# Scores right behind the values' products, gates' parts ahead of the last copies, first tiles and shared weights handed over earlier

## The reference

```
x = x + tanh(g_xattn) * mlstm(layernorm(x), ctx, ctx)
x = x + tanh(g_ffn)   * experts(layernorm(x))

mlstm (16 heads of 32):
    ig = [q,k,v] @ Wi + bi ;  fg = [q,k,v] @ Wf + bf
    log_D = cumsum(log_sigmoid(fg)) differences + ig   (lower triangle)
    D  = exp(log_D - rowmax(log_D))
    C  = (q k^T / sqrt(32)) * D
    h  = C / max(|sum C|, exp(-rowmax)) @ v ; normalised per head, times ln_scale

experts: scores = sqrt(softplus(x @ gate_w^T)), the two best of 16 per token,
    y = w1*E_a(x) + w2*E_b(x) + shared(x),  E(x) = (silu(x W1^T) * (x W3^T)) W2^T
```

## Time and profile before

| | |
|---|---|
| median of 3 runs | 775.14 us (774.03 to 776.44) |
| the profiled execution, its own time | 775.68 us |
| its span, first to last instruction | 773.9 us |
| PE busy | 691.8 us (89%) |
| DVE, ACT, POOL busy | 506.0, 411.1, 392.3 us |
| mean granted TensorE clock | 0.974 |
| front stage, to its barrier | up to about 85.5 us |
| attention | up to about 299 us |
| mixture | the rest |

### The profile page before, as it was taken

How to read it: one execution, slowest core, us unless ns; L and a number is a source line. 1 busy time by engine, 2 the same in 40 slices (tenths; PEclk the granted TensorE clock), 3 DMA queues, 4 the chain that set the end, 5 groups by cost and what they waited for, 6 DMA issues and landing times.

```text
span 773.9 us, 19573 instructions
## 1 busy us (share of the span) xinstructions
PE 691.8 (89%) x7407; PEld 603.0 (78%) x7408; DVE 506.0 (65%) x1007; ACT 411.1 (53%) x851; POOL 392.3 (51%) x592
## 2 busy tenths in 40 slices
PE   0877498899899887999999999999999999999994
PEld 0644377777777766778899998999999999999993
DVE  4758278987777698866259795534566676766650
ACT  0667467686766674434362332223466656666651
POOL 2410377888888774521112542223355766667554
PEclk9999699999999998999999999999999999999998
DMA  7885464446555710687633222423678888979864
GB/s 248 276 277 173 120 191 142 155 143 183 143 161 168 229 41 28 203 303 277 236 104 110 59 86 75 118 88 105 200 223 237 226 257 229 238 225 240 256 130 54
DMA packets 90212, 134.55 MB, mean 174 GB/s; under 512 B 16704, under 2 KB 43840, under 8 KB 90144
## 3 DMA queue, kind: packets, MB, share of 16 engines
q1 hardware_dynamic: 73472, 106.04, 42.9%
q0 software_dynamic: 7168, 17.04, 11.1%
q10 hardware_dynamic: 9504, 10.55, 4.4%
HBM read 92.06 MB, written 33.95 MB: 163 GB/s over the span
## 4 chain that ended last, share of the span: by engine, by line
PE 68%; DVE 8%; ACT 4%; DMA 4%; issue 3%; POOL 1%; SPq 0%; ACTq 0%; POOLq 0%; DVEq 0%
PE psH L1302 30%; PE psY L1322 15%; PE psQ L719 4%; PE ring L736 4%; PE psO L764 4%; PE ring L704 2%; PE ring L730 2%; ACT dec L806 2%; PE psT L1282 2%; DMA out<-ystage,sidx 1%; DMA xT<-over13l 1%; DVE dec L886 1%; PE psR L1349 1%; DVE xl L1551 1%; ACT sq L830 1%
## 5 line engine op out<-in xcount | busy, mean ns | idle before, releaser
L1302 PE MATMUL psH<-xh,w13h 128*128 128x256 f32 (+1 forms) x768 | 220.8, 288 | 2.8 <-issue 2.8
L1302 PE MATMUL psH<-xh,w13l 128*128 128x256 f32 (+1 forms) x768 | 215.5, 281 | 0.0
L1302 PE MATMUL psH<-xl,w13h 128*128 128x256 f32 (+1 forms) x768 | 215.1, 280 | 0.0
L1794 POOL TENSOR_TENSOR hl<-sg,hh 128x256 fp32r<-128x256 f32 (+1 forms) x96 | 79.5, 837 | 177.9 <-ACT hh L1425 177.4
L1302 PEld LDWEIGHTS psH<-xh,w13h 128*128 128x128 f32 (+1 forms) x768 | 138.0, 180 | 11.3 <-issue 10.4
L1302 PEld LDWEIGHTS psH<-xl,w13h 128*128 128x128 f32 (+1 forms) x768 | 138.3, 180 | 0.8
L1302 PEld LDWEIGHTS psH<-xh,w13l 128*128 128x128 f32 (+1 forms) x768 | 138.0, 180 | 0.0
L886 DVE SCALAR_TENSOR_TENSOR dec<-psQ,dec 128x512 f32<-128x512 f32 x128 | 79.5, 683 | 44.2 <-PE psQ L719 44.1
L1420 ACT ACTIVATE sg<-psH 128x256 f32<-128x256 f32 (+1 forms) x96 | 36.4, 379 | 126.0 <-PE psH L1302 125.3
L1557 DVE TENSOR_TENSOR sg<-sg,psH 128x256 f32<-128x256 f32 (+1 forms) x96 | 40.0, 416 | 95.4 <-ACT sg L1420 95.4
L806 ACT ACTIVATE dec<-ring 128x512 f32<-128x512 f32 x128 | 71.2, 596 | 17.6 <-PE ring L707 17.1
(11 more groups left out here) (228 smaller groups left out, 1410.5 us busy)
## 6 DMA issues: line engine op xcount, KB each, us to landing
raw<-w13T SPq DMA_DIRECT2D x64, 352.0 KB, 4.4
gcT<-ctxT ACTq DMA_DIRECT2D x8, 1024.0 KB, 6.1
kT<-ctxT SPq DMA_DIRECT2D x16, 512.0 KB, 4.2
ctxs<-ctx SPq DMA_DIRECT2D x16, 512.0 KB, 3.8
xn<-xnorm SPq DMA_DIRECT2D x16, 512.0 KB, 3.3
out<-xres SPq DMA_DIRECT2D x16, 512.0 KB, 4.9
raw<-w2T SPq DMA_DIRECT2D x16, 512.0 KB
qst<-qT_all SPq DMA_DIRECT2D x14, 512.0 KB, 5.0
```

What stands on the lines that cost most here:

```text
L1302: last = nc.tensor.matmul(psH[m][0:n, v, :], w[wp][:, c, col:col + n], x[xp][:, c, :], start=(c == 0 and k == 0), stop=(c == DC - 1 and k ...
L1794: nc.gpsimd.tensor_tensor(hs[u.p][1][0:n, m, :], sg[0:n, m, :], hs[u.p][0][0:n, m, :].bitcast(F32), ALU.subtract).then_inc(hl_ready, 1)
```

## The change

Three places change.

1. In the front stage's last pair VectorE, not ScalarE, copies `xT`, and the copies to `qT_all` come after VectorE's last gate steps. ScalarE makes its second part ahead of the sums and the third ahead of the last `keep`. SyncE's last `store` follows the saving of all parts. VectorE alone fills both masks.
2. In attention `queries` comes right behind `values`, then `gather_state`, then the decays 2 and 3. The lists of the other engines stay.
3. At the end of attention SyncE starts the shared expert's quarters one at a time, at five places of sequences 13 to 15, where before all six transfers went out together. TensorE turns the first tile ahead of the last `values` and the second behind it, ahead of the last `back`. ScalarE and VectorE follow: VectorE normalises the first two tiles one step earlier and the next two after its last `take`.

```
@@ front_stage
+            for out, rows in ((g.aml[1], maskl), (g.amr[1], maskr)):
+                copy(out[:, :, :], rows[:, :].rearrange("p (o t) -> p o t", o=1).broadcast_to([P, NH, P]))
...
-            for n, _ in enumerate(gates_saved(sp, gt, half, 0, d)):
-                if n == 1:
-                    store(sp, 7)
+            for _ in gates_saved(sp, gt, half, 0, d):
+                pass
+            store(sp, 7)
...
-                    dve.wait_ge(xt_ready, n + 1)
+                    dve.wait_ge(turned, n + 1)
+                    dve.wait_ge(projected, n - 1)
+                    nc.vector.tensor_copy(xT[k][:, :, :], psT[k][:, :, :]).then_inc(xt_ready, 1)
+                for _ in gates:
+                    pass
+                for k in range(2):
+                    n = 2 * p + k
                     nc.vector.tensor_copy(g.qT_all[:, (n - 2) * DC:(n - 1) * DC, :], psT[k][:, :, :])
...
-                second_set(dve, nc.vector.tensor_copy, g.amr[1], maskr)
+                second_set(dve, nc.vector.tensor_copy)
@@ attention_stage, sync
                 load_em(b)
+                if b > B - 3:
+                    next(more)
...
                     sp.wait_ge(q_in[1], 16 * (B // 2 - 2))
+                if b >= B - 3:
                     next(more)
@@ attention_stage, tensor
                     values(i, r - 1, bank(r, OUT))
+                queries(i, r)
+                if r % 2 == 1:
+                    gather_state(i, r)
                 for k in range(2):
                     ring_free(use(last2(r) + k))
                     decay(i, r, 2 + k, bank(r, last2(r) + k))
-                    if k == 0:
-                        if r % 2 == 1:
-                            gather_state(i, r)
-                        queries(i, r)
...
             i, r = LAST
+            pe.wait_ge(c_done, 4 * NT)
+            next(more)
             ring_free(uses(i, r, END))
@@ mixture_stage, sync
                     sync.dma_start(raw13[:, c, :], src).then_inc(w_in[c], 16)
+                    if wset == 0:
+                        yield
@@ mixture_stage, vector
-            for count, quarters in ((2, ()), (2, ()), (0, (0, 1)), (2, (2,)), (2, (3,))):
+            for count, quarters in ((2, ()), (2, ()), (2, (0, 1)), (0, (2,))):
                 side.issue(-1, count)
                 split13(early(0), quarters)
-                if quarters == (3,):
-                    for j in range(2):
-                        split_x(early(0), j)
-                yield
+                yield
+            split13(early(0), (3,))
+            for j in range(2):
+                split_x(early(0), j)
+            yield
+            side.issue(-1, 2)
```

40 lines of the change are left out of this document (18 added, 22 removed).

## The result

The changed kernel takes 777.98 us (median of 6 runs, 777.33 to 781.73), the kernel before 776.02 beside it (6 runs, 774.03 to 778.89). The ratio on record is 1.0057, with a 95% interval of 1.0031 to 1.0083: **slower by 4.4 us**, between 2.4 and 6.4, where 2.95 us less was forecast. It is not the quotient of the two medians, which lie only 2.0 us apart. The median of 777.98 is outside the range of 769.0 to 776.5. In what follows ratios are turned into us in the same way, and each carries an uncertainty of about 2 us; the lengths of single steps in the traces are far sharper.

A forecast was written before the change was run, and what follows sets the result against it. TensorE, without gaps after 331 us, was taken as the bound, earlier gains arriving one to one: -4.5 + 4.45 - 2.7 - 0.2 = -2.95 us against 775.68; the median, 0.54 lower, gives 772.2 us, range 769.0 to 776.5.

The forecast's parts named there:

- Front end, -4.5: Front stage's end: masks saved and ready at 80.95 instead of 85.44 us, a gain of 4.5 us.
- Even steps, "so nothing": Attention's even steps: scores ahead of the decays start VectorE about 0.44 us earlier, nothing waits for it, so no change.
- Odd steps, +0.6 each: Attention's odd steps: state's sums behind the scores delay ScalarE's copies, 0.6 us more each, 5.4 over nine steps.
- First step, -0.75: Attention's very first step: scores no longer wait for a quarter of decays, which takes 0.7 there; gain 0.75 us.
- Weights, -2.7: Shared expert's weights near sequence 14: loading by quarters removes a 1.15 us wait and 1.6 of slow clock, gain 2.7 us.
- Rival (c): Weights' loads: decays still land late or the load moves beside other transfers, losing the 2.7 gain: 774.9 us; chance 0.17.
- Hand-over, -0.2: End of attention to the experts: late weighings against a faster way to `xl`, net gain 0.2 us, 1.7 if the clock holds.
- then 0.9 for the tiles: VectorE's first two normalisations at the end of attention, after waiting for GpSimd's power: priced at 0.9 us for both.
- The faster way from values 31 to the first `psH`: Tail: first tile turned and split under the last `values`; second `xl` ends at 298.05 in place of 299.2, -1.1 us.
- the clock falls behind the long gap: TensorE ahead of chunk 30's `values`: idle for 2.6 us, after which its clock falls to 1.2 GHz.
- Rival (b), the clock falls inside attention: Attention's odd steps: gaps grow to 1.2 us and each clock fall costs 1.6; four falls give 778.6 us; chance 0.07.
- The rule that the forecast set against this part: TensorE in attention: short idle times with PSUM banks in rotation can move the clock, so odd steps lose over 0.6 us.

The follow-up runs named there:

- `odd_gather_first`: The changed kernel with hand-over and even steps as before, and the state's sums right behind `values` in odd steps: ratio 0.9979 to the kernel before.

## Why the prediction was wrong, point by point

- **Front end, -4.5:** right, -4.5 measured alone (-2.8 to -6.2), and 4.7 at the end of the masks over all traces; by the steps that were named.
- **Even steps, "so nothing":** wrong, +1.4. The corner's product had been free beside the scores, a cost that the forecast put at nothing.
- **Odd steps, +0.6 each:** mechanism and size right: 5.0 for 5.4, 1.0 for 0.9, 0.66 for 0.45. Steps 29 and 31, left out, add 0.2.
- **First step, -0.75:** right in sign, 0.45. With this and the even steps the order adds up to +5.8 by the traces and +6.1 by the runs, and not +4.45.
- **Weights, -2.7:** in the trace exactly so, but on average 1.3 alone, and nothing beside the earlier front end. The term was read from one execution of a disturbance that came out between nothing and 3.8 us. Rival (c) named this loss, for a wrong reason: the decays do land in time.
- **Hand-over, -0.2:** the step that failed is "then 0.9 for the tiles": 2.64 beside GpSimd's wide instructions. That is 1.7 us more than it was priced at, and the weighing starts 3.85 us later, not 2.0. The faster way from values 31 to the first `psH` was right (4.77 us for 8.78), but with the late weighings `psH` comes 0.7 us late against values 29 in the changed kernel and not 1.1 early. With the hand-over alone values 31 are 5.2 us late against values 29, and 2.2 of this is given back by the last instruction. Net +3.0 in that trace, +2.6 by the runs. That the clock falls behind the long gap was right.
- **Rival (b), the clock falls inside attention:** did not happen; it is 1.00 in all stretches from 97 to 284 that I read. The rule that the forecast set against this part (the Trainium skill, TensorE: Matmul & The Clock Gate, A second HAM failure mode: psum-queue depth-cycling) decided nothing: TensorE's gap ahead of `values` did not double (0.65 us at 199.71 for 0.58 at 199.96), a second one of 0.44 came ahead of `back` instead, and at such gaps the clock held. Where a gap was longer, 1.72 us in step 7 of `odd_gather_first`, it did fall in the middle of attention.
- The signs of what was missed agree: +1.65 for the order, +1.4 for the weights, +2.8 for the hand-over, 5.9 in all. The forecast of 772.2 was 5.8 below the median; measured by the ratio (4.4 for -2.95) it missed by 7.3, which with the intervals is the same. None of it was in the range, since each term was given its own bounds but the sum was taken as if they would not all fall on one side.

What stays open: whether the order really costs more inside the change (7.4 us) than alone (6.1), why the kernel with 30 added products is not faster, and what decides, from run to run, when the clock of steps 0 and 1 comes back and whether it falls behind the same wait of 2.2 us at the end of attention.

## What to carry to other kernels

Where an engine's list is strict, first ask which product its longest unbroken stretch waits for, and put that one first: the same change with the state's sums ahead of the scores is 1.2% faster than without. An instruction moved into another stage takes the neighbours that it finds there; look at what GpSimd runs there before using the old duration of a VectorE instruction. And a stall that stands in one trace is one draw: read the same place in several executions before it becomes a term of a sum.

## What the runs showed of the hardware

- VectorE's normalisation of 128x512 fp32 (two scalars per row): 0.50 us beside GpSimd's narrow instructions or none, 1.32 beside its tensor instructions of 496 and 512 columns (changed kernel), 1.19 beside one of 1024 and then one of 256 (kernel before, 311.81). GpSimd's power of 128x4: 1.02 us with VectorE idle, 1.66 beside VectorE's 128x704 split.
- A product that uses the last 32 rows of TensorE's array runs beside the next one that uses the first 32: 0.11 us for each such pair, 1.4 net over the even steps.
- The granted clock stays at 1.0 from 80 to 93 us when an idle stretch of 6.4 us is filled with useless products (0.5 without), yet the kernel is not faster (1.0026): the clock fell behind the next gap of 1.11 us.
- The same wait of TensorE, 2.17 to 2.26 us ahead of values 31, was followed by a granted clock of 0.50 in three traces and of 1.00 in four.
